# Attention of the second layer in units of two heads by 128 queries, on half-size tiles of the matrix engine

## What is computed

```python
# B, S, D, H, A = 4, 512, 128, 16, 64 in the kernel's terms; all weights fp32
q = einsum("bsd,hda->bsha", xn, Wq) + bq
k = einsum("bsd,hda->bsha", xn, Wk) + bk
v = einsum("bsd,hda->bsha", xn, Wv) + bv
scores = einsum("bqha,bkha->bhqk", q, k) / sqrt(A)     # key > query masked
out = einsum("bhqk,bkha->bqha", softmax(scores), v)
s = einsum("bqha,had->bqd", out, Wo) + bo
```

## Times and profile before

| | |
|---|---|
| median of 3 runs | 5986.1 us (5985.38 to 5986.49) |
| the profiled execution, its span | 5995.4 us (no other time is recorded for it) |
| busy in the span: PE, PE loads | 4804.1 us (80%), 3412.1 us (57%) |
| DVE, ACT, POOL | 3795.6 (63%), 3211.5 (54%), 1986.0 (33%) |
| attention of the second layer | from about 973 to 1583 us of the span |
| one batch's softmax loop in it | 1024 to 1128 us |

### The profile page before, as it was taken

One profiled execution on the slowest core, in us unless ns is written; L12 is line 12 of the kernel. 1 busy time (PEld: TensorE's weight loads), 2 busy tenths in 40 slices (PEclk: granted clock), 3 DMA queues, 4 the chain that ended last, 5 costly groups with the idle time before them and its releaser, 6 DMA issues. The chain is left out here.

```text
span 5995.4 us, 91995 instructions
## 1 busy us (share of the span) xinstructions
PE 4804.1 (80%) x27408; PEld 3412.1 (57%) x27408; DVE 3795.6 (63%) x8398; ACT 3211.5 (54%) x9294; POOL 1986.0 (33%) x1579
## 2 busy tenths in 40 slices
PE   6888897999864446888888888888888887688888
PEld 4667664666631104566666666666666665466666
DVE  5555223444558886777777777777777776455522
ACT  4444343555323335666666766666766665244433
POOL 3333100222204553444444444444444442122200
PEclk8888998999975558999999999999999999688899
DMA  0000000000000001000000000000000000000000
GB/s 16 1 2 2 33 0 19 2 2 2 13 3 0 0 0 47 1 0 21 0 0 21 0 0 21 0 0 21 0 0 0 0 0 1 16 1 0 0 28 7
DMA packets 26030, 41.55 MB, mean 7 GB/s; under 512 B 12208, under 2 KB 18376, under 8 KB 25160
## 3 DMA queue, kind: packets, MB, share of 16 engines
q1 hardware_dynamic: 25800, 38.86, 1.9%
HBM read 36.75 MB, written 2.10 MB: 6 GB/s over the span
## 5 line engine op out<-in xcount | busy, mean ns | idle before, releaser
L1380 PE MATMUL ps<-l2f_wqkv,l2f_xsT 128*128 (+3 forms) x1536 | 741.6, 606 | 96.5 <-DVE xnT L1575 90.5
L1312 POOL TENSOR_TENSOR l2f_rn<-l2f_ss,neghalf 128x16 f32<-128x16 f32 x192 | 564.7, 2941 | 436.2 <-DVE l2f_ss L1569 436.2
L1757 ACT ACTIVATE l2f_p<-ps,l2f_negmax 128x96 f32<-128x96 f32 x1536 | 501.7, 339 | 281.8 <-DVE l2f_negmax L1600 278.2
L1318 POOL TENSOR_TENSOR l2f_cosd<-xnT,l2f_rot 128x1024 f32<-128x1024 f32 x192 | 487.0, 2541 | 174.8 <-DVE xnT L1575 174.8
L1438 PE MATMUL ps<-l2f_pT,l2f_vw 96*128 96x128 f32 x3072 | 419.7, 280 | 39.2 <-DVE l2f_pT L1622 38.9
L1380 PEld LDWEIGHTS ps<-l2f_wqkv,l2f_xsT 128*128 128x128 f32 (+1 forms) x1536 | 243.4, 178 | 347.4 <-issue 197.2
L1772 ACT COPY l2f_oT<-ps 64x256 f32<-64x256 f32 x768 | 281.3, 366 | 268.1 <-PE ps L1438 256.4
L1438 PEld LDWEIGHTS ps<-l2f_pT,l2f_vw 96*128 96x128 f32 x3072 | 379.4, 194 | 59.4 <-issue 54.2
L1338 POOL TENSOR_TENSOR l2f_rstd<-l2f_mv,neghalf 128x1 f32<-128x1 f32 x96 | 52.8, 550 | 1045.9 <-DVE l2f_mv L1634 1045.9
L1411 PEld LDWEIGHTS ps<-l2f_kT,l2f_qz 128*128 128x128 f32 x3072 | 398.3, 194 | 1.5 <-issue 0.4
L1411 PE MATMUL ps<-l2f_kT,l2f_qz 128*128 128x96 f32 x3072 | 397.9, 273 | 0.0
(11 more groups left out here) (348 smaller groups left out, 12274.8 us busy)
## 6 DMA issues: line engine op xcount, KB each, us to landing
l2f_wqkv<-L_ffn_Wqkv_dram SPq DMA_DIRECT2D x18, 512.0 KB
l0f_w<-L_w_dram SPq DMA_DIRECT2D x2, 2304.0 KB
l3f_w<-L_w_dram SPq DMA_DIRECT2D x2, 2048.0 KB
l2f_wo<-L_ffn_Wo_dram SPq DMA_DIRECT2D x6, 512.0 KB
l2f_w<-L_ffn_W_dram SPq DMA_DIRECT2D x6, 341.0 KB
l2f_b<-L_ffn_b_dram SPq DMA_DIRECT2D x6, 341.0 KB
l1f_w<-L_w_dram SPq DMA_DIRECT2D x1, 1152.0 KB
k_turn<-l3a_kF SPq DMA_DIRECT2D x4, 256.0 KB, 2.0
```

Source lines behind the costliest of these rows:

```text
L1312: nc.gpsimd.tensor_tensor(rn[:, k], ss[:, k], g.neghalf[:, 0:HEADS], ALU.pow).then_inc(rn_ready, 1)
L1318: nc.gpsimd.tensor_tensor(cosd[:, k].rearrange("p (h d) -> p h d", d=DH), nrm[:, k].rearrange("p (h d) -> p h d", d=DH), rot[:, k, 0, t].u ...
L1380: ins = nc.tensor.matmul(g.ps[0:rows, 2 * (k % 2) + hf], x, wqkv[:, bass.ds(weight_slot(it), 1), c0 + hf * 512:c0 + (hf + 1) * 512] .rearr ...
L1757: ins = nc.scalar.activation(p[:, n % 2, c], g.ps[:, 4, c * KW:(c + 1) * KW], ACT.Exp, bias=negmax[:, col:col + 1], accum_out=rowsum[:, co ...
```

## The change

- A unit of the new class PairSoftmax is two heads by 128 queries; 4 units per pair, 32 per batch, with 128, 256, 384 or 512 keys. p, pT, the maxima and sums have a dimension for the head.
- q is kept as it comes (qT, one ACT copy per pair); no zeros, no L708 and L709. Head h's scores are a product over rows 64h to 64h+63 only, into bank 2*(n%2)+h, in pieces of at most 256 keys, head 0 and head 1 in turn. Before them comes the mask, a product of the identity with a bf16 triangle of 128 columns for each head.
- One maximum, one reciprocal and one POOL multiplication serve both heads; exp stays one per head; each head's turned tile has its own bank (three in turn, 4 to 6) and its own DVE copy.
- Outputs: each head's v, 64 columns, gives rows 64h to 64h+63 of bank 7; one ACT copy takes them out.
- In `tensor` PE is given, per unit n: scores n+2, outputs n-1, transposes n. In `vector` DVE is given: reciprocal n, maximum n+2, copies n-1.
- The mask causal64 becomes causal128, loaded once. Other stages keep the class Softmax.

```diff
+class PairSoftmax:
+    TURN_BANK, TURN_BANKS, PV_BANK = 4, 3, 7
...
+    def pe_scores(self, pe, b, n):
+        pe.wait_ge(self.probs_ready, self.at(b, 0 if n < 2 else n if self.big(n) else n - 1))
+        pieces = self.pieces(n)
+        if self.mask_before is not None:
+            pieces = [(nk - P, nk)] + [(c0, min(c1, nk - P)) for c0, c1 in pieces if c0 < nk - P]
+            for h in range(2):
+                nc.tensor.matmul(s[:, h, nk - P:nk], self.g.identb[:], self.mask_before, start=True, stop=False)
...
+        for i, (c0, c1) in enumerate(pieces):
+            for h in range(2):
+                ins = nc.tensor.matmul(s[:, h, c0:c1], self.q(n, h), self.k(n, h, c0, c1),
+                                       start=self.mask_before is None or i > 0, stop=c1 <= m0 or self.mask_before is not None)
...
+    def pe_pv(self, pe, b, n):
+        pe.wait_ge(self.copied[0], self.at(b, n + 1))
+        pe.wait_ge(self.copied[1], self.at(b, n + 1))
...
+        for c in range(chunks):
+            for h in range(2):
+                ins = self.nc.tensor.matmul(self.g.ps[self.lane(n, h), self.PV_BANK, 0:P], self.v(n, h, c),
+                                            self.pT[:, n % 2, h, c * P:(c + 1) * P],
+                                            start=(c == 0), stop=(c == chunks - 1))
...
+    def tensor(self, pe, b):
+        self.pe_scores(pe, b, 0)
+        self.pe_scores(pe, b, 1)
+        for n in range(self.units):
+            self.pe_scores(pe, b, n + 2)
+            self.pe_pv(pe, b, n - 1)
+            self.pe_turn(pe, b, n)
+        self.pe_pv(pe, b, self.units - 1)
...
+    def vector(self, dve, b):
+        self.maximum(dve, b, 0)
+        self.maximum(dve, b, 1)
+        for n in range(self.units + 2):
+            if n < self.units:
+                self.inverse_sum(dve, b, n)
+            self.maximum(dve, b, n + 2)
+            if 1 <= n <= self.units:
+                for h in range(2):
+                    if self.copiers[h] == "dve":
+                        self.copy_turned(dve, self.nc.vector.tensor_copy, b, n - 1, h)
...
@@ l1_attn_stage @@
-        qz = sb("qz", [P, PAIRS, SEQ // QB, 2, QB])
+        qT = sb("qT", [P, PAIRS, SEQ])
...
+        at = PairSoftmax(g, sb, sem, units=PAIRS * TILES, keys=lambda n: P * (n % TILES + 1), lane=lane,
+                         q=lambda n, h: qT[lane(n, h), n // TILES, n % TILES * P:(n % TILES + 1) * P],
+                         k=lambda n, h, c0, c1: kT[lane(n, h), n // TILES, c0:c1],
+                         v=lambda n, h, c: v[:, c, head(n, h)], mask_before=g.causal128[:], mask_after=None,
+                         collect=collect, collector="act", every=1, copiers=("dve", "dve"))
...
-            nc.vector.memset(at.p[:], 0.0)
-            nc.vector.memset(qz[:], 0.0).then_inc(zeroed, 1)
...
-            act.wait_ge(zeroed, 1)
...
-                        for hf in range(2):
-                            rows = slice(hf * DH, (hf + 1) * DH)
-                            ins = nc.scalar.activation(qz[rows, c, :, hf], g.ps[rows, i % 2].rearrange("p (i q) -> p i q", q=QB),
-                                                       ACT.Identity, bias=bq[rows, c:c + 1], scale=DH ** -0.5)
+                        ins = nc.scalar.activation(qT[:, c], g.ps[:, i % 2], ACT.Identity, bias=bq[:, c:c + 1],
+                                                   scale=DH ** -0.5)
```

More of the change, by code:

```diff
@@ L86, in load_stage @@
         sb, sem, _ = scope(nc, stack, "load")
-        masks = sb("masks", [P, 72])
+        masks = sb("masks", [P, P + 8])
         landed = sem("landed")
@@ L94, in _ @@
             sp.dma_start(g.ident[:], g.c["ident"]).then_inc(landed, 16)
-            sp.dma_start(masks[:, 0:64], g.c["causal64"]).then_inc(landed, 16)
-            sp.dma_start(masks[:, 64:72], g.c["causal8"]).then_inc(landed, 16)
+            sp.dma_start(masks[:, 0:P], g.c["causal128"]).then_inc(landed, 16)
+            sp.dma_start(masks[:, P:P + 8], g.c["causal8"]).then_inc(landed, 16)
             sp.wait_ge(landed, 64)
@@ L103, in _ @@
             nc.vector.tensor_copy(g.identb[:], g.ident[:])
-            nc.vector.tensor_copy(g.causal64[:], masks[:, 0:64])
-            nc.vector.tensor_copy(g.causal8[:], masks[:, 64:72])
+            nc.vector.tensor_copy(g.causal128[:], masks[:, 0:P])
+            nc.vector.tensor_copy(g.causal8[:], masks[:, P:P + 8])
 def norm_stage(g, tag):
@@ L326 @@
+PIECE = 256
 class OutProduct:
@@ L621, in l1_attn_stage @@
     HD = HEADS * DH
-    QB = 64
-    BLOCKS = SEQ // QB
     with ExitStack() as stack:
@@ L637, in l1_attn_stage @@
         bq_scaled = once("bq_scaled")
-        zeroed = once("zeroed")
         xb_ready = sem("xb_ready")
@@ L646, in collect @@
         def collect(act, b, n):
-            c, i = n // BLOCKS, n % BLOCKS
+            c, t = n // TILES, n % TILES
             if n == 0:
@@ L650, in collect, with lane, head @@
             act.wait_ge(at.pv_done, at.at(b, n + 1))
-            for hf in range(2):
-                rows = slice(hf * DH, (hf + 1) * DH)
[L653 to L660, removed]
+            nc.scalar.copy(oT[:, c, t * P:(t + 1) * P], g.ps[:, at.PV_BANK, 0:P]).then_inc(at.collected, 1)
+        def lane(n, h):
+            return slice(h * DH, (h + 1) * DH)
+        def head(n, h):
+            return slice((2 * (n // TILES) + h) * DH, (2 * (n // TILES) + h + 1) * DH)
+        at = PairSoftmax(g, sb, sem, units=PAIRS * TILES, keys=lambda n: P * (n % TILES + 1), lane=lane,
[3 more added lines that the diff above has]
+                         collect=collect, collector="act", every=1, copiers=("dve", "dve"))
         block = stack.enter_context(nc.Block())
@@ L2345, in four_gated_layers @@
         g.identb = sb("identb", [P, P], BF16)
-        g.causal64 = sb("causal64", [P, 64], BF16)
+        g.causal128 = sb("causal128", [P, P], BF16)
         g.causal8 = sb("causal8", [P, 8], BF16)
@@ L2370, in constants @@
     heads = (i[:, None] // (D // HEADS) == np.arange(HEADS)[None]).astype(np.float32)
-    return {"ident": np.eye(P, dtype=np.float32), "causal64": causal(64), "causal8": causal(8), "heads": heads,
+    return {"ident": np.eye(P, dtype=np.float32), "causal128": causal(P), "causal8": causal(8), "heads": heads,
             **more_constants()}
```

127 lines of the change are left out of this document (added).

## The result

The changed kernel took 6258.55 us (median of 4 runs, 6251.11 to 6259.0) against 5986.3 us: ratio 1.0442, 95% interval 1.0426 to 1.0458 (the two medians alone give 1.0455, inside it). It is slower by 272 us. The forecast was 6198 with a range of 6085 to 6330, for the reason that proved true; it put PE's own work too high and the price of the clock too low, two errors in opposite directions.

A forecast was written before the change was run, and what follows sets the result against it. PE bounded the loop at 13.0 us per pair; taking turns with DVE makes it 18.5 (+177 us), the clock adds 65, projection -22, start -8: +212 on 5986.1, so 6198 us, range 6085 to 6330.

The forecast's parts named there:

- The wait: Softmax loop: PE's outputs wait for DVE's copies behind its maximum in each of 128 units, about 220 us in all.
- 6.5 + 0.6: Loop, us per pair: DVE's maxima and copies less overlaps 6.5; restart of PE (signal and unhidden load) 0.6.
- The fixed part of the sum: Loop, per pair: masks, two shape changes, last product's latency, maxima and copies, PE's restart, transposes: 12.6 us.
- S and O: Loop, PE per pair: scores S 3.6 us, outputs O 2.3; bounds 4.5 each in series, 2.25 each side by side.
- for 128-column pieces loads alone fill the time: Scores: a load lasts as long as 128 columns stream, so only 256-column pieces gain from two tiles: 3.6 us.
- The clock: Loop: clock falls to 0.85 as PE stands; PE's 11.4 us grow by 2.0 per pair, +65 us in all.
- between them 0.62 gives 0.8: Loop: clock for PE busy share 0.62, read between windows with 0.94 at 72% busy and 0.57 at 49%.
- Outside the loop: Projection: one 0.69 us copy fewer per pair, -22 us; start: no zero fills, -8 us.
- C: Rival, loop: full overlap of the tiles and full clock, 17.1 us per pair, 6087 us; chance 0.17.
- B: Rival, loop: fp32 tiles not side by side, 21.6 us per pair warm, clock about 0.9, 6282 us; chance 0.29.
- D: Rival, loop: copies ready before outputs, PE's work alone counts, 10.0 us per pair, 5860 us; chance 0.05 including other savings.

The follow-up runs named there:

- The first experiment: The changed kernel with DVE's copies of n-1 moved ahead of its maximum of n+2: 5949.68 us, ratio 0.9927 to the kernel before.
- The run at full clock: The changed kernel with 4 to 10 unused bf16 products per unit between scores and outputs: 6074.19 us, ratio 1.0132 to the kernel before.
- g1_whole_array_scores: The run at full clock with each head's q padded with zeros to K = 128, scores on the whole array: 6144.04 us against 6074.19.

## Why the prediction was right, and where it was off

- **The wait.** Right: scores, maximum, two copies, outputs in one thread, in every unit; 210 us of PE waits where about 220 were named. PE stood 6.8 us per pair where 6.5 + 0.6 were forecast. The first experiment shows that the order is the cause, the order alone on the old kernel shows it again.
- **The fixed part of the sum.** 12.6 us per pair was forecast beside S and O. The run at full clock has 16.2 less 4.4 for both = 11.8. The 0.8 us lie in the masks and the change of shape behind them: from the masks' start to the scores' start it takes 0.20 us a unit (1199.01 to 1199.21 above), 0.8 per pair, where 0.8 for the masks and 0.8 for the changes were taken. With scores on the whole array, where that change is missing, it takes 0.11 (1210.03 to 1210.14 in g1_whole_array_scores), so this change costs 0.09 us and not 0.2, and the two masks of a unit 0.11 and not 0.2.
- **S and O.** 3.6 + 2.3 = 5.9 was taken; about 2.2 + 2.2 is what the runs show. At full clock 12 score instructions of 512 keys (8 of 128 columns, 4 of 256) took 1.15 us where the whole array takes 1.97, and 16 output instructions 1.09 us where 15 x 0.113 + 0.28 = 1.97 would be their series. The failing step is "for 128-column pieces loads alone fill the time": it took the loads of the two tiles to share one path, but they overlap as the products do. The Trainium skill (TensorEngine Tiling (Array Packing), Key Properties) says that they do; g1_whole_array_scores agrees, with 17.75 against 16.2 us.
- **The clock.** 0.85 was taken, 0.55 to 0.63 was granted; 2.0 us per pair was forecast, 5.8 measured. The failing step is the interpolation "between them 0.62 gives 0.8", and the raise to 0.85 after it went the wrong way. The busy share alone does not tell the clock: the changed loop shows 70% busy at 0.55, the old projection 72% at 0.94, and the old kernel in the new order 70% at 0.76. One thing that differs is how the standing is spread: 0.6 us at a time between the pairs of the projection, up to 1.3 us in the old kernel in the new order, up to 2.3 us here. No run varied this by itself, so the cause stays open; and it isn't all, for the changed kernel's first two batches stood alike, 54 us each and 2.3 us at most, and were granted 0.63 and 0.55. A busy share that is measured at the low clock also flatters, since the same products take longer (8 outputs 1.12 us against 0.66).
- **The two errors** met in part: 18.5 + 2.0 = 20.5 us per pair against 16.3 + 5.8, measured together as 22.05. The difference, 1.5 x 32 = 50 us, is most of the 60 us by which 6198 was short. That the time fell well inside the range is in part luck: with PE's work put right and the clock left as taken, the forecast would have been 16.2 + 2.0, about 6122 us; with the clock put right and the work left, 18.5 + 5.8, about 6320.
- **Outside the loop.** -30 forecast, -28 measured. The period of the projection and the start in the profile after (q of one pair, then of the next; first ACT copy):

```profile
1205.82 1.10 PE L894 MATMUL ps<-l1a_xb,l1a_wq 128*128 128x512 f32 x2
1206.76 1.12 PE L894 MATMUL ps<-l1a_xb,l1a_wk 128*128 128x512 f32 x2
1207.72 1.10 PE L894 MATMUL ps<-l1a_xb,l1a_wq 128*128 128x512 f32 x2
```

```profile
988.02 1.28 ACT L934 ACT_TABLE_LOAD   x1 [12.09 <-DVE l1a_bq L911]
990.06 0.69 ACT L934 ACTIVATE l1a_qT<-ps,l1a_bq 128x512 f32<-128x512 f32 x1 [0.75 <-PE ps L894]
```

  1.90 us per pair in place of 2.59, and ACT begins 2.1 us after the first product starts (987.95), not 11.5.
- **Rivals.** C had the tiles right and the clock wrong (its 6087 is near the 6074 of the run at full clock), B the time about right (6282) for a wrong reason: serial tiles at clock 0.9. That a rival with the wrong cause came nearest in time is a warning about judging a theory by its total. D was wrong on this kernel, but its 5860 is near what the units reach once the order is mended, 5899.

## What to carry to other kernels

When two engines' lists each contain an item that feeds the other, write them side by side and ask of each wait what stands ahead of its releaser in the other's list; here one line too early turned a maximum of two engines' times into their sum. Stalls of TensorE that recur every few microseconds must be priced with the clock on top: here, with stalls of 1.7 us on average and 2.3 at most, the clock cost 5.8 us per pair, about as much as the turns themselves (up to 5.4), and products that nobody reads paid for themselves. Stalls of 0.6 us cost little of it in the old projection (0.94). A change that brings several things is to be split before it is judged: this one held a 1.7% gain, once the order was mended and the outputs had a second bank.

## What the hardware showed that was not expected

- The granted clock was 0.55 at 70% busy and 1.00 once 28 filler products per pair stood in the gaps, and the filled program was 184 us faster. The Trainium skill (TensorE: Matmul & The Clock Gate, HAM oscillation) tells of idle gaps between bursts of products that take the clock down each time. The trace agrees that gaps do so, but the gap in the page's example, a wait for a DMA, is longer than any here: no stall in these loops was over 2.3 us.
- Weight loads and products of two half tiles overlap fully also for fp32, whose product is two instructions: 12 instructions in 1.15 us against 1.97 on the whole array.
- TensorE starts instructions of another tile ahead of up to three older ones: listed head by head, 8 output instructions took 1.13 us, as when listed in turn (1.12), but 16 took 2.85 against 1.97.
- The granted clock is not fixed by the list of instructions and its stalls: the four batches of the changed kernel stood 54 us each and had 0.63, 0.55, 0.61 and 0.61.
